# A soft threshold of two VectorE instructions added to the end of the quantiser of the last layer

## The chip, the cores and the metric

One Trainium2 chip, eight cores, one launch. Every core runs the same program on its own batch element; no core waits for another inside the program. The metric is the device time of the slowest core in microseconds.

## The reference

Two layers are applied to x of shape (8, 4096, 1024) in float32, each of them an attention part and a feed-forward part with a layernorm ahead and a residual behind. The change touches the last part alone, the quantised feed-forward of layer 1:

```
def act_quant(x):
    scale = 127.0 / jnp.clip(jnp.max(jnp.abs(x), axis=-1, keepdims=True), 1e-05)
    return jnp.clip(jnp.round(x * scale), -128, 127) / scale
def weight_quant(w):
    scale = 1.0 / jnp.clip(jnp.mean(jnp.abs(w)), 1e-05)
    return jnp.clip(jnp.round(w * scale), -1, 1) / scale
def bit_linear(x, w):
    return jnp.einsum('bsd,hd->bsh', act_quant(x), weight_quant(w))   # forward value

h = bit_linear(x, w1)                       # 1024 -> 4096
h = silu(depthwise_conv1d(h, conv_w, conv_b))   # 3 taps over the sequence
return bit_linear(h, w2)                    # 4096 -> 1024
```

Ahead of it run a gated delta-rule attention, two blocks of local attention with a GELU feed-forward, and an attention over 64 summary tokens. They make up 43.4 ms of the 48.3 and are not touched.

## The kernel before, in words

The activation lies transposed in SBUF, `xf`, 8 chunks of 128 channels by 4096 tokens. The program is a long sequence of blocks; inside a block each engine has its own queue, and the hand-over from one engine to the next goes by counting semaphores: `tick` (a drain and an increment, line 142 stands for the increment of every engine), `wv`, `wt`, `ws` (wait for all that VectorE, TensorE or ScalarE has announced so far) and `wdma` (the same for the DMAs). `b.dma` issues one DMA and then makes the issuing queue wait until it has landed, so there is one DMA in flight on each of the two queues that issue any (SyncE and GpSimd). VectorE runs its own instructions in order, and `v.drain()` between two of them holds the second until the first has left the pipeline.

`_quant7` (lines 2041 to 2055) rounds one 128 by 512 tile. It scales the tile (L2043 by a tile, L2045 by a column), adds and subtracts three large constants (L2047, L2048, L2049), adds and subtracts two of the results (L2051, L2053), and clamps into `out` (L2055). It has three callers in `stage_l1_ffn`, and they run one after the other:

- The weights: for w1T 8 chunks of 8 tiles, for w2T 32 chunks of 2 tiles, 128 calls in all. SyncE loads a chunk into `wch`, for which it waits until VectorE is done with the last one; VectorE quantises all its tiles in place and casts the chunk into the one buffer `wq16s` (L2224); GpSimd stores it to `wr1` or `wr2`. VectorE waits for both the load and the last store before it begins a chunk.
- The activation: 8 windows of 512 tokens, 8 tiles in each, 64 calls, in place in `xf`. Behind them `xf` is cast to bf16 (L2282 to L2287), and the first matrix product with its convolution follows (L2311 to L2360), which writes `ybuf`.
- The hidden layer: 8 windows of 512 tokens, 32 tiles in each, 256 calls. SyncE loads a tile of `ybuf` into one of two buffers, GpSimd loads 128 rows of `wr2` into one of two buffers `w2sl`, VectorE quantises into one of two halves of `yq` in bf16, TensorE does 8 products of 128x128 by 128x512 (L2437) into 8 PSUM banks. VectorE may write a half of `yq` only when the products of two tiles ago are done, and GpSimd has the same rule for `w2sl`. After 32 tiles 8 blocks are scaled, added to the residual and stored (L2461, L2463).

Of the kernel before, what the change touches and what calls it, by code (L numbers as in the profile page):

```python
# [12 lines left out]
ALU = mybir.AluOpType  # L13
# [2024 lines left out]
        b.tick(v, b.sem_v)  # L2038


def _quant7(b, v, w, t1, t2, out, lo, hi, scale_tile=None, scale_col=None):
    if scale_tile is not None:
        v.tensor_mul(w, w, scale_tile)  # L2043
    else:
        v.tensor_scalar(w, w, scale_col, None, ALU.mult)  # L2045
    v.drain()  # L2046
    v.tensor_scalar(t1, w, MAGIC2, MAGIC2, ALU.add, ALU.subtract)  # L2047
    v.tensor_scalar(t2, w, MAGIC3, MAGIC3, ALU.add, ALU.subtract)  # L2048
    v.tensor_scalar(w, w, MAGIC1, MAGIC1, ALU.add, ALU.subtract)  # L2049
    v.drain()  # L2050
    v.tensor_add(w, w, t1)  # L2051
    v.drain()
    v.tensor_sub(w, w, t2)  # L2053
    v.drain()
    v.tensor_scalar(out, w, lo, hi, ALU.max, ALU.min)  # L2055


def stage_l1_ffn(b, xf):
# [143 lines left out]
    for wi, (wname, nch_, cols_, scol, wrh) in enumerate((  # L2202
            ("L1_ffn_w1T", 8, 4096, z.s1col, wr1),
            ("L1_ffn_w2T", 32, 1024, z.s2col, wr2))):
        with nc.Block() as blk:
            for ch in range(nch_):
                @blk.sync
                def _(sy, ch=ch, wname=wname, cols_=cols_):
                    g = b.sg.get("wch", 0)
                    if g:  # L2210
                        sy.wait_ge(b.sem_v, g)
                    b.dma(sy, wch[:, 0:cols_],
                          hb[wname].ap()[ch * 128:(ch + 1) * 128, :])

                @blk.vector
                def _(v, ch=ch, cols_=cols_, scol=scol):
                    b.wdma(v)
                    b.wdma(v, b.sem_g)
                    for sub in range(cols_ // U):
                        _quant7(b, v, wch[:, sub * U:(sub + 1) * U], t1, t2,  # L2220
                                wch[:, sub * U:(sub + 1) * U], -1.0, 1.0,
                                scale_col=scol)
                        v.drain()
                    v.tensor_copy(wq16s[:, 0:cols_], wch[:, 0:cols_])  # L2224
                    b.tick(v, b.sem_v)
                    b.sg["wch"] = b.C.get(b.sem_v)

                @blk.gpsimd
                def _(gp, ch=ch, cols_=cols_, wrh=wrh):
                    b.wv(gp)  # L2230
                    b.dma(gp, wrh.ap()[ch * 128:(ch + 1) * 128, :],
                          wq16s[:, 0:cols_], b.sem_g)
# [6 lines left out]
    for w in range(NCH):  # L2239
        t0 = w * W  # L2240
        with nc.Block() as blk:
# [16 lines left out]
            @blk.vector  # L2258
            def _(v, t0=t0):
                v.tensor_scalar(sct, sct, 1e-5, None, ALU.max)  # L2260
                v.drain()
                v.reciprocal(sct, sct)
                v.drain()
                v.tensor_scalar(sct, sct, 127.0, None, ALU.mult)
                v.drain()
                v.reciprocal(z.mu[:, t0:t0 + W], sct)
                v.drain()
                v.tensor_scalar(z.mu[:, t0:t0 + W], z.mu[:, t0:t0 + W],
                                z.m1col, None, ALU.mult)
                v.drain()  # L2270
                for cc in range(NCH):
                    sl = xf[:, cc * T + t0:cc * T + t0 + W]
                    _quant7(b, v, sl, qt1, qt2, sl, -128.0, 127.0,
                            scale_tile=sct)
                    v.drain()
                b.tick(v, b.sem_v)
# [106 lines left out]
    for w in range(NCH):  # L2383
        t0 = w * W
        with nc.Block() as blk:
# [14 lines left out]
            for hc in range(32):  # L2400
# [18 lines left out]
                @blk.vector  # L2419
                def _(v, hc=hc, bufp=bufp):  # L2420
                    b.wdma(v)
                    g = b.sg.get(("yq", bufp), 0)
                    if g:
                        v.wait_ge(b.sem_t, g)
                    _quant7(b, v, ystg[bufp], qt1b, qt2b,
                            yq16[:, bufp * W:(bufp + 1) * W], -128.0, 127.0,
                            scale_tile=scw)
                    b.tick(v, b.sem_v)
                    b.sg[("ystg", bufp)] = b.C.get(b.sem_v)
# [178 lines left out]
```

How the kernel before makes its waits and increments, by code:

```python
    def dma(self, eng, dst, src, sem=None):  # L131
        sem = self.sem_w if sem is None else sem
        eng.dma_start(dst, src).then_inc(sem, 16)
        self.C.add(sem, 16)
        eng.wait_ge(sem, self.C.get(sem))
# [1 line left out]
    def wdma(self, eng, sem=None):  # L137
        sem = self.sem_w if sem is None else sem
        eng.wait_ge(sem, self.C.get(sem))
# [5 lines left out]
    def wt(self, eng):  # L145
        eng.wait_ge(self.sem_t, self.C.get(self.sem_t))
# [1 line left out]
    def wv(self, eng):  # L148
        eng.wait_ge(self.sem_v, self.C.get(self.sem_v))
# [1 line left out]
    def ws(self, eng):  # L151
        eng.wait_ge(self.sem_s, self.C.get(self.sem_s))
# [257 lines left out]
            @blk.sync  # L410
            def _(sy, wname=wname, j=j, bufp=bufp, sidx=sidx):
                if sidx >= 2:
                    sy.wait_ge(b.sem_t, C.get(b.sem_t) - 1)
                b.dma(sy, slab3(z.wslab, bufp * NCH * 128, NCH, 128),
                      wslab_src(hb[wname], j * 128, 128))
# [342 lines left out]
            @blk.sync  # L758
            def _(sy, j=j, bufp=bufp):
                if j >= 2:
                    sy.wait_ge(b.sem_t, C.get(b.sem_t) - 1)
                b.dma(sy, slab3(z.wslab, bufp * NCH * 128, 4, 128),
                      wslab_src(hb["L0_attn_Wgu"], j * 128, 128))
# [77 lines left out]
            @blk.sync  # L841
            def _(sy, j=j, bufp=bufp):
                if j >= 2:
                    sy.wait_ge(b.sem_t, C.get(b.sem_t) - 1)
                b.dma(sy, slab3(z.wslab, bufp * NCH * 128, NCH, 128),
                      wslab_src(hb["L0_attn_Wo"], j * 128, 128))
```

## Time and profile before

| | us |
|---|---|
| median of the runs of before (two: 48318.64 and 48483.29) | 48400.96 |
| the profiled execution's own time | 48304.51 |
| its span, slowest core (core 2) | 48302.2 |
| spans of all eight cores | 47419.8 to 48302.2 |
| stretch up to the last feed-forward part | 0 to about 43420 |
| quantising the weights | 43614.5 to 44390 |
| quantising the activation | 44390 to 44882 |
| first product and convolution | 44882 to 46782.6 |
| quantising the hidden layer, second product, store | 46782.6 to 48302 |

The profile shows one execution of one core. Busy time is the time in which an engine ran an instruction; the value in square brackets behind a row of the timeline is how long the engine stood idle just before it, with what released it. The time between the starts of two rows that follow each other without such a bracket is the cost of the first one together with its drain.

### The profile page before, as it was taken

The page shows a single profiled execution, that of the slowest core. Times are in us where ns is not written, and L with a number is a line of the kernel's source. Part 1 is how long each engine was busy: PE and PEld are TensorE (multiplying, and loading weights), DVE is VectorE, ACT ScalarE, POOL GpSimd, SP SyncE. Part 2 cuts the span into 40 slices and gives each one's busy share as a digit, 9 for nine tenths or more (in the row PEclk, how much of TensorE's full clock was granted, in tenths as well). Part 3 has the DMA queues.
Part 4 walks back from the last instruction along what each step waited for, and adds up shares of the span by engine and source line. Part 5 has one row for each costly group of instructions (what it writes and reads, how often), then busy time and mean ns, then how long its engine had stood idle before and what let it go on. Part 6 is the DMA issues. An engine that isn't in the chain of part 4 may idle for free. (4 is left out here: it accounts for less than half of the span.)

```text
span 48302.2 us, 310408 instructions; the slowest of 8 cores (47419.8 to 48302.2 us)
## 1 busy us (share of the span) xinstructions
PE 29041.8 (60%) x118094; PEld 17414.8 (36%) x118176; DVE 9809.4 (20%) x17093; ACT 5842.3 (12%) x7328; POOL 230.0 (0%) x420
## 2 busy tenths in 40 slices
PE   5556555655555555577777655557788766640334
PEld 3444444444431111166566211115666642110111
DVE  1222222222122111100000111110000012226556
ACT  0110111111111121211111121111111110000000
POOL 0000000000000000000000000000000000000001
PEclk6666666666666666677877666667777776665666
DMA  1001000000010000033333100002323320011013
GB/s 40 23 20 32 19 25 29 18 28 25 20 35 15 14 10 16 9 84 84 89 84 85 36 11 13 13 11 68 82 79 81 85 82 28 26 54 53 34 59 110
DMA packets 3348641, 2085.22 MB, mean 43 GB/s; under 512 B 169190, under 2 KB 3236075, under 8 KB 3333868
## 3 DMA queue, kind: packets, MB, share of 16 engines
q1 hardware_dynamic: 3309804, 1847.23, 13.8%
q0 software_dynamic: 37376, 218.13, 1.1%
q8 instruction: 963, 15.78, 0.1%
q14 instruction: 498, 4.08, 0.0%
HBM read 1914.11 MB, written 150.99 MB: 43 GB/s over the span
## 5 line engine op out<-in xcount | busy, mean ns | idle before, releaser
L1589 PE MATMUL ps<-pool 128*128 128x256 f32 x11264 | 3962.5, 528 | 2116.5 <-DVEq L142 2116.5
L1589 PEld LDWEIGHTS ps<-pool 128*128 128x128 f32 x11264 | 2966.3, 270 | 3118.8 <-issue 2494.6
L423 PE MATMUL ps<-pool 128*128 128x256 f32 x7168 | 2805.2, 575 | 1458.5 <-DVEq L142 1458.5
L1642 PE MATMUL ps<-pool 128*128 128x256 f32 (+1 forms) x11264 | 3005.8, 433 | 258.7 <-DVEq L142 258.7
L1595 PE MATMUL ps<-pool 128*128 128x256 f32 x11264 | 2927.8, 420 | 0.0
L423 PEld LDWEIGHTS ps<-pool 128*128 128x128 f32 x7168 | 2137.8, 305 | 2127.0 <-issue 1629.7
L1642 PEld LDWEIGHTS ps<-pool 128*128 128x128 f32 (+1 forms) x11264 | 2405.4, 218 | 861.2 <-issue 470.0
L1320 PE MATMUL ps<-pool 128*64 128x256 f32 (+3 forms) x1920 | 1174.8, 712 | 2406.9 <-ACTq L142 2406.9
L1595 PEld LDWEIGHTS ps<-pool 128*128 128x128 f32 x11264 | 2359.5, 209 | 448.1
L1614 DVE SCALAR_TENSOR_TENSOR pool<-ps,pool 128x256 f32<-128x256 f32 x704 | 340.0, 483 | 8326.2 <-ACTq L142 8326.2
L1308 ACT ACT_TABLE_LOAD x960 | 1231.7, 1283 | 5450.4 <-DVEq L142 5450.4
L1607 ACT ACT_TABLE_LOAD x704 | 903.2, 1283 | 7833.6 <-PE ps L1595 7833.6
L1127 PE MATMUL ps<-xf,pool 128*128 128x512 f32 (+1 forms) x2048 | 1322.2, 789 | 618.3 <-DMA pool<-L_ffn_wqkv 376.8
L647 PE MATMUL ps<-pool 64*64 64x64 f32 x10240 | 924.0, 293 | 823.3 <-ACTq L142 673.0
L1320 PEld LDWEIGHTS ps<-pool 128*64 128x64 f32 x1920 | 255.6, 189 | 3144.3 <-issue 3144.3
L2311 PE MATMUL ps<-xq,wsl 128*128 128x512 bf16 x2007 | 623.9, 464 | 1229.8 <-DMA wsl<-wr 1004.7
L197 PE MATMUL ps<-cst_c_id,pool 64*64 64x64 f32 x2560 | 783.1, 306 | 840.3 <-PEq L467 347.9
L1292 PE MATMUL ps<-pool 64*128 64x256 f32 (+3 forms) x1920 | 1205.0, 722 | 129.0 <-DVEq L142 129.0
L198 PE MATMUL ps<-cst_c_id,pool 64*64 64x64 f32 x5120 | 1198.5, 336 | 0.0
L1323 PE MATMUL ps<-pool,cst_c_onescols 128*1 128x256 f32 (+3 forms) x1920 | 1156.8, 704 | 0.0
L647 PEld LDWEIGHTS ps<-pool 64*64 64x64 f32 x10240 | 838.5, 196 | 870.0 <-issue 870.0
L2437 PE MATMUL ps<-yq,w2sl 128*128 128x512 bf16 x2007 | 653.2, 480 | 823.9 <-DVEq L142 728.5
(333 smaller groups left out, 30493.0 us busy)
## 6 DMA issues: line engine op xcount, KB each, us to landing
pool<-L_ffn_w SPq DMA_DIRECT2D x1344, 512.0 KB
pool<-L_ffn_w SPq DMA_DIRECT2D x256, 1344.0 KB
pool<-L_attn_Wq SPq DMA_DIRECT2D x192, 512.0 KB
pool<-L_attn_Wo SPq DMA_DIRECT2D x192, 512.0 KB
pool<-L_attn_Wk SPq DMA_DIRECT2D x136, 512.0 KB
pool<-L_attn_Wv SPq DMA_DIRECT2D x136, 512.0 KB
pool<-L_ffn_wqkv SPq DMA_DIRECT2D x128, 512.0 KB
ybuf<-pool POOLq DMA_DIRECT2D x32, 2048.0 KB, 6.6
```

Of the source, the lines that this page charges most:

```text
L198: return t.matmul(out_ps, src, cid[64:128, 64:128], start=True, stop=True, tile_position=(64, 64))
L423: ins = t.matmul(z.ps_p[:, 0:LT], z.wslab[:, bufp * NCH * 128 + cc * 128:bufp * NCH * 128 + (cc + 1) * 128], z.xn[:, cc * LT:(cc + 1) * LT ...
L647: ins = t.matmul(z.ps_a[PR(h), CB(p)], prevp[PR(h), CB(p)], prevt[PR(h), CB(p)], start=True, stop=True, tile_position=(64 * h, 64 * h))
L1127: ins = t.matmul(out, lh, rh, start=(i == 0), stop=(i == len(mms) - 1))
L1292: ins = t.matmul(pss[:, 0:qn], lhs, rhs, start=True, stop=True)
L1308: s.activation(z.at[:, 0:qn], pss[:, 0:qn], AF.Exp, bias=cst["c_onescols"][:, 4:5])
L1320: t.matmul(z.ps_o[64 * hh:64 * hh + 64, q0:q0 + qn], vsl, z.at[:, 0:qn], start=(kci == 0), stop=last, tile_position=(0, 64 * hh))
L1323: ins = t.matmul(psd[0:1, q0:q0 + qn], cst["c_onescols"][:, 0:1], z.at[:, 0:qn], start=(kci == 0), stop=last)
L1589: t.matmul(z.ps_s0[0:n, 0:ST], wb[:, cc * 128:cc * 128 + n], xn2[:, cc * ST:(cc + 1) * ST], start=(cc == 0), stop=(cc == NCH - 1))
L1595: ins = t.matmul(z.ps_s1[0:n, 0:ST], wb[:, 1024 + cc * 128:1024 + cc * 128 + n], xn2[:, cc * ST:(cc + 1) * ST], start=(cc == 0), stop=(cc ...
L1607: s.activation(z.gsc[0:n, 0:ST], z.ps_s1[0:n, 0:ST], AF.Gelu, bias=z.b1gcol[0:n, lyr * 22 + j:lyr * 22 + j + 1])
L1642: ins = t.matmul(z.ps_o[:, 0:ST], wb[0:n, j * 128:j * 128 + 128], h1sl(j, ST)[0:n, :], start=(j == 0), stop=(j == NJ - 1))
```

## The change

`_quant7` ends in three instructions instead of one. The clamp to lo and hi no longer writes `out` but the work tile `w`. A second clamp of `w`, to plus and minus 2^-14, goes into the scratch tile `t1`, and `out` becomes the difference of the two. Each of the two instructions added has a drain ahead of it. Nothing else is changed: no buffer, no DMA, no wait, no call.

```
+QEPS = 6.103515625e-05
+
+
 def _quant7(b, v, w, t1, t2, out, lo, hi, scale_tile=None, scale_col=None):
@@
     v.tensor_sub(w, w, t2)
     v.drain()
-    v.tensor_scalar(out, w, lo, hi, ALU.max, ALU.min)
+    v.tensor_scalar(w, w, lo, hi, ALU.max, ALU.min)
+    v.drain()
+    v.tensor_scalar(t1, w, -QEPS, QEPS, ALU.max, ALU.min)
+    v.drain()
+    v.tensor_sub(out, w, t1)
```

## Rows read from the trace of the kernel before

**Rows 1.** Page, part 1: busy time (share of the span) xinstructions.

```profile
PE 29041.8 (60%) x118094; PEld 17414.8 (36%) x118176; DVE 9809.4 (20%) x17093; ACT 5842.3 (12%) x7328; POOL 230.0 (0%) x420
```

**Rows 2.** Windows of core 2: stretch, length, busy us (instructions), clock, DMA share, GB/s.

```profile
43614.50:44390.00 775.50, 0.00 (x0) 0.00 (x0) 475.12 (x936) 0.00 (x0) 21.53 (x40) 0.50 0.20 65
44390.00:44882.00 492.00, 39.94 (x112) 16.67 (x112) 399.95 (x658) 0.00 (x0) 0.00 (x0) 0.50 0.00 0
46782.60:48302.00 1519.40, 653.17 (x2007) 213.91 (x2048) 1075.93 (x1960) 0.00 (x0) 178.36 (x320) 0.69 0.37 111
```

**Rows 3.** Timeline of VectorE, weights: start, length, instruction, idle before it.

```profile
43987.99 0.42 DVE L2049 TENSOR_SCALAR pool<-pool 128x512 f32<-128x512 f32 x1
43988.48 0.69 DVE L2051 TENSOR_TENSOR pool<-pool 128x512 f32<-128x512 f32 x1
43989.25 0.69 DVE L2053 TENSOR_TENSOR pool<-pool 128x512 f32<-128x512 f32 x1
43990.01 0.43 DVE L2055 TENSOR_SCALAR pool<-pool 128x512 f32<-128x512 f32 x1
43990.51 0.69 DVE L2224 CAST wq16s<-pool 128x1024 bf16<-128x1024 f32 x1
43996.10 0.48 DVE L2045 TENSOR_SCALAR pool<-pool 128x512 f32<-128x512 f32 x1 [4.89 <-DMA wr<-wq16s]
```

**Rows 4.** Instruction groups of VectorE by form: count, busy us, mean ns, idle before.

```profile
L2053 DVE TENSOR_TENSOR pool<-pool 128x512 f32<-128x512 f32 x384 | 265.9, 692 | 29.6 <-issue 1.3
L2055 DVE TENSOR_SCALAR yq<-pool 128x512 bf16<-128x512 f32 x256 | 109.2, 427 | 20.2 <-issue 0.9
L2055 DVE TENSOR_SCALAR pool<-pool 128x512 f32<-128x512 f32 x128 | 54.6, 427 | 10.5 <-issue 0.9
L2055 DVE TENSOR_SCALAR xf<-xf 128x512 f32<-128x512 f32 x64 | 27.3, 427 | 4.9
L1963 DVE TENSOR_SCALAR xf<-ps,pool 128x512 f32<-128x512 f32 x64 | 48.0, 750 | 543.0 <-PE ps L1953 543.0
```

**Rows 5.** Waits of VectorE in the weights: waited for, us in total, times, longest.

```profile
DVE pool L2045 <- DMA wr<-wq16s: 227.8, 38, 11.2
DVE pool L2055 <- issue: 0.9, 2, 0.4
```

**Rows 6.** Timeline of VectorE, hidden layer, one tile.

```profile
46841.48 0.69 DVE L2043 TENSOR_TENSOR pool<-pool 128x512 f32<-128x512 f32 x1 [0.26 <-issue]
46844.96 0.43 DVE L2055 TENSOR_SCALAR yq<-pool 128x512 bf16<-128x512 f32 x1
46845.64 0.69 DVE L2043 TENSOR_TENSOR pool<-pool 128x512 f32<-128x512 f32 x1 [0.26 <-issue]
```

**Rows 7.** Waits of VectorE in the hidden layer, all eight windows.

```profile
DVE pool L2461 <- DMA outT<-pool: 206.7, 56, 4.8
DVE pool L2043 <- issue: 64.4, 245, 0.6
DVE pool L2461 <- PE ps L2437: 27.4, 8, 4.1
DVE pool L2043 <- PE ps L2437: 2.2, 7, 0.5
```

**Rows 8.** Timeline of GpSimd in the hidden layer: its loads of the weights.

```profile
46883.07 0.55 POOL L133 DMA_DIRECT2D w2sl<-wr  x1 [3.85 <-DMA w2sl<-wr]
46887.21 0.55 POOL L133 DMA_DIRECT2D w2sl<-wr  x1 [3.59 <-DMA w2sl<-wr]
...
46904.31 0.55 POOL L133 DMA_DIRECT2D w2sl<-wr  x1 [3.80 <-DMA w2sl<-wr]
```

**Rows 9.** Timeline of TensorE in the hidden layer: two tiles.

```profile
46908.29 1.89 PE L2437 MATMUL ps<-yq,w2sl 128*128 128x512 bf16 x8 [2.27 <-DVEq L142]
...
46920.77 3.57 PE L2437 MATMUL ps<-yq,w2sl 128*128 128x512 bf16 x8 [1.40 <-DVEq L142]
```

## Prediction

> **What bounds the kernel now.** I read the totals first [rows 1]: TensorE is busy 60% of the span and VectorE 20%. From that alone two more VectorE instructions per tile would look free. The total is a mean over parts with different limits, though, and the change lives in one part only, so the second view is the table of windows, cut where the three callers of `_quant7` begin and end [rows 2]. There the picture is reversed. While the weights are quantised TensorE runs nothing in 775.5 us and VectorE is busy for 475. While the activation is quantised VectorE is busy 400 of 492 us. In the hidden layer VectorE is busy 1076 of 1519 us and TensorE 653. Together the three stretches are 2787 us, 5.8% of the span, and all that the change can do happens in them.
>
> The third view is what VectorE waits for inside each.
>
> Weights: a quantising instruction follows the last one at the drain's distance, then comes the cast, then VectorE stands 4.9 us until the store of that cast has landed [rows 3]. Such waits are 227.8 us over 38 chunks [rows 5]. The store begins when the cast is done, the next quantising begins when the store is done, and the load of the next chunk too is let go only by the cast. So compute, store and compute again stand in a row; nothing runs beside VectorE that would hide a longer chunk.
>
> Activation: no DMA moves at all in that stretch [rows 2], and TensorE only takes part between the windows. It is one chain on VectorE.
>
> Hidden layer: here four queues work side by side, and this is the one place where cover could exist. One tile takes VectorE 4.16 us, from L2043 at 46841.48 to L2043 at 46845.64 [rows 6]. GpSimd's load of `w2sl` comes round in 4.25 us: from 46883.07 to 46904.31 there are 5 steps [rows 8]. TensorE's eight products take 1.89 us at the one clock level and 3.57 at the other, and otherwise it sits waiting for VectorE's tick [rows 9]. VectorE and GpSimd are thus almost even. What decides is which of them waits: VectorE waited for TensorE (through which a late `w2sl` would reach it) for 2.2 us in all [rows 7]. The 0.26 us of idle time ahead of each L2043 has "issue" as its cause, 64.4 us over 245 tiles [rows 7]: the tick and the waits that are already fulfilled. VectorE sets the pace.
>
> **The change, part by part.** It removes nothing: the clamp L2055 stays, with another destination. In the two f32 callers that is the same shape and type as before. In the hidden layer it writes f32 to `pool` in place of bf16 to `yq`; the rows of L2055 show 427 ns for each of the three forms [rows 4], so that edit costs nothing.
>
> It adds a clamp f32 to f32 with constants as limits, the same operation as L2055: 0.427 us. With its drain the distance between two starts is 43990.51 - 43990.01 = 0.50 us [rows 3].
>
> It adds a subtraction of two SBUF tiles. L2053 is just that, 692 ns [rows 4], and with its drain 43990.01 - 43989.25 = 0.76 us [rows 3]. For 192 of the 448 calls it is the same form. For the 256 calls of the hidden layer it writes bf16, a form that has no row. Bounds: at best it runs like the clamp, whose time is the same with bf16 out, 427 ns; at worst like the slowest 128x512 operation that is not a reciprocal, 750 ns with a PSUM source [rows 4]. I take 692, because two f32 sources is what sets L2053 apart from L2055, and a bf16 destination changed nothing for L2055. The ends for the range: 256 x (0.427 - 0.692) = -68 us and 256 x (0.750 - 0.692) = +15 us.
>
> The Trainium skill has a rule for it ("VectorE: DVE Perf Modes", What auto-detection actually checks): the packed two-element mode wants every tensor to be 16-bit, so a subtraction with f32 sources stays at one element a cycle. By that rule the sum is the one that I take; no run here shows it yet.
>
> Per call, from the means: 0.427 + 0.692 busy, and a gap of (29.6 - 1.3)/384 = 0.074 and (20.2 - 0.9)/256 = 0.075 us for the two drains [rows 4], 1.268 us. The starts give 0.50 + 0.76 = 1.26.
>
> - Weights, 128 calls: 162 us. All on the path, for the reason above. Waiting behind VectorE are the store on GpSimd's queue and the load on SyncE's; they are late by the same amount and no longer in themselves.
> - Activation, 64 calls: 81 us, all on the path.
> - Hidden layer, 256 calls: 325 us. A tile goes from 4.16 to 5.43 us. What is late is the tick of `yq`; TensorE, which has 0.6 to 2.3 us to spare per tile, gets more idle time. GpSimd gets 5.43 - 4.25 = 1.18 us of slack per load. SyncE's load of `ybuf` lands while VectorE is at the other buffer. The tail of each window (the last products, eight scaled blocks and stores) is not touched.
>
> Sum: 448 x 1.268 = 568 us.
>
> Small terms: pauses of 0.4 us with "issue" as cause come now and then, ten in the 936 instructions of the weights, of which two stand in [rows 5]. With 256 more instructions there and 512 in the hidden layer this adds some 2 us. At the end of each window VectorE waits for the last products, 27.4 us in eight windows, 4.1 at the longest [rows 7]. The products there run now at the one clock level and now at the other (1.89 us is that of 2.4 GHz, 3.57 that of 1.2) [rows 9], and TensorE will be less busy, 653 us over some 1844 in place of 1519. If the granted clock stays at the lower level throughout, each tail takes the 4.1 us: 8 x 4.1 - 27.4 = 5 us. I take 3.
>
> Sum with them: 573 us. The profiled execution took 48304.5, which gives 48878. The median of the runs is 96 us above that execution and would give 48974. I forecast the middle, 48926 us, a ratio of 1.011 to 1.012 to before.
>
> **Rivals.**
>
> *The subtraction into bf16 runs at the clamp's rate.* For it speaks that nothing in this trace shows the form; against it that L2053's price comes with two sources and not with its destination. 573 - 68 = 505 us: 48858.
>
> *The hidden layer was not bound by VectorE.* For it speaks that GpSimd's 4.25 us is no shorter than VectorE's 4.16; a load at 4.25 would hide 0.09 us a tile at once, 23 us. If each of the 0.26 us ahead of L2043 [rows 6] was in truth a wait for that chain, 64 us of the addition vanish in it: 48862. To hide it all the chain would have to be 5.43 us long, which no row of GpSimd or TensorE is. That would leave 162 + 81 = 243 us: 48597. Against it: 2.2 us of waits for TensorE [rows 7].
>
> *The store and load queue of GpSimd gets slower and becomes the bound (slower by over 2%).* The place is the load of `w2sl` in the hidden layer. Its price is nothing up to a period of 5.43 us, and 256 us for each microsecond beyond that. 2% is 968 us, so 395 us must come on top of 573, and the period would have to reach 6.97 us where it is 4.25. The added clamp is one more instruction of 0.43 us a tile beside it; if it pushed every load back by its whole length, the period would be 4.68 us, and still nothing is late. Time at the deciding point: 49369.
>
> The Trainium skill describes that mechanism ("SBUF — State Buffer", SBUF: two separate sides): while VectorE runs a clamp of this kind GpSimd can't write descriptors, so its DMA starts late. By that rule the loads would be later by up to one clamp, and with the period worked out above the time would stay 48926.
>
> *The subtraction or the clamp is not free of surprises in the drains.* Every drain in the rows costs 0.07 to 0.08 us. At twice that in both, 448 x 0.15 = 67 us more: 48993.
>
> **How the numbers follow.** The forecast has 0.86, the bf16 rate 0.05, a partly or wholly covered hidden layer 0.04, dearer drains 0.03, the GpSimd chain or another doubling of the cost 0.02. The range goes from the cheaper sums on the lower basis to the dearer on the upper one. The low end is 48304.5 + 505 = 48810, less some 20 for the scatter. The high end is 48483.3 (the higher of the two runs) + 573 = 49056, with 15 for a slower subtraction and some 30 for drains: 49100. What is left out is about 1 in 10. 2% is about what a measurement of this kernel can tell from no change, and that is 968 us; the sum is 1.2%, so the case within 2% has 0.96, slower by more 0.03, faster by more 0.01.
>
> **What the profile after would show.** L2055's successor at 427 ns in all three callers; a new TENSOR_SCALAR line x448 at 420 to 427 ns; a new TENSOR_TENSOR line x448 at 692 ns, x256 of them with bf16 out (at 427 the first rival holds). VectorE's total rises by 448 x 1.119 = 501 us to 10311. The three stretches grow by 162, 81 and 325 us, and everything ahead of 43614 keeps its time. The waits for `wr<-wq16s` stay near 228 us and those for `outT` near 207. A tile of the hidden layer takes 5.43 us. I am wrong if VectorE shows new waits for TensorE or DMA there, if the tile stays under 5.2 us, or if the time outside the three stretches moves by more than the runs differ among themselves.

## The result and the profile after

The changed kernel takes 48839 us in the median, the one before 48417; over the runs that can be compared the ratio is 1.0099, with a 95% interval of 1.0061 to 1.0136. So it is slower by about 1%, and less than 2%. The profiled execution of the changed kernel has a span of 48873.3 us, 571 us more than that of before.

First the totals on the page of the changed kernel, the part with the busy times:

```profile
PE 29184.4 (60%) x118176; PEld 17459.6 (36%) x118176; DVE 10314.5 (21%) x17989; ACT 5844.2 (12%) x7328; POOL 232.7 (0%) x420
```

Against [rows 1] VectorE has 896 instructions more, twice 448, and 505 us more of busy time. At 20% and 21% of the span this line alone would never tell that the kernel became slower by it.

The windows of its slowest core (core 1) over the same three stretches; columns as in [rows 2]:

```profile
43637.00:44567.40 930.40, 0.00 (x0) 0.00 (x0) 617.86 (x1193) 0.00 (x0) 20.98 (x39) 0.50 0.16 54
44567.40:45143.00 575.60, 39.95 (x112) 16.73 (x112) 471.56 (x788) 0.00 (x0) 0.54 (x1) 0.50 0.00 1
47027.20:48873.30 1846.10, 790.40 (x2048) 240.43 (x2048) 1363.91 (x2472) 0.00 (x0) 181.05 (x320) 0.62 0.30 91
```

The groups of VectorE for the instructions that are new or have a new destination:

```profile
L2062 DVE TENSOR_TENSOR yq<-pool 128x512 bf16<-128x512 f32 x256 | 177.2, 692 | 19.9 <-issue 0.9
L2060 DVE TENSOR_SCALAR pool<-pool 128x512 f32<-128x512 f32 x384 | 166.0, 432 | 30.6 <-issue 1.3
L2058 DVE TENSOR_SCALAR pool<-pool 128x512 f32<-128x512 f32 x384 | 164.1, 427 | 30.7 <-issue 1.7
```

L2058 is the old clamp, L2060 the clamp to 2^-14, L2062 the subtraction. The subtraction into bf16, the form that had no row before, takes 692 ns like the one into f32.

The end of a call in the weights, VectorE's timeline, to be read against [rows 3]:

```profile
44565.09 0.69 DVE L2056 TENSOR_TENSOR pool<-pool 128x512 f32<-128x512 f32 x1
44565.86 0.43 DVE L2058 TENSOR_SCALAR pool<-pool 128x512 f32<-128x512 f32 x1
44566.36 0.43 DVE L2060 TENSOR_SCALAR pool<-pool 128x512 f32<-128x512 f32 x1
44566.86 0.69 DVE L2062 TENSOR_TENSOR pool<-pool 128x512 f32<-128x512 f32 x1
44567.63 0.69 DVE L2231 CAST wq16s<-pool 128x1024 bf16<-128x1024 f32 x1
```

0.50 us from L2060 to L2062 and 0.77 from there to the cast are what a call got longer by.

A window cut by hand cuts instructions. For the comparisons from here on the stretches are measured on each core from the start of the first VectorE instruction of one part to that of the next: first tile of the weights, first maximum of the activation (L2248), copy ahead of the first product (L2282), first scale of the hidden layer (L2389), end. The means over eight cores, us:

| | until the weights | weights | activation | product, convolution | hidden layer |
|---|---|---|---|---|---|
| before | 43298 | 770.8 | 484.5 | 1850.5 | 1518.5 |
| changed | 43425 | 927.1 | 565.5 | 1856.4 | 1843.5 |
| difference | +127 | +156.3 | +81.0 | +5.9 | +325.0 |

The three stretches grow by 562 us. The other two columns are where the scatter sits. In the profiles below the first one has means from 42708 to 43883 us with the same code in it, its cores from 41723 to 44215, and it goes with TensorE's mean granted clock over the whole span: 0.70 on the cores that are there after 41.7 ms and 0.654 on one that takes 44.2. The 562 us are thus known to some ten microseconds from the stretches, while the ratio of whole runs, 1.0099, has an interval of 295 to 658 us at 48417. The sum of the stretches is inside it. Whole times of single runs below say little for the same reason, and in some of them the cores of one die ran at a lower clock, so the stretches are what is compared.

What VectorE waited for in the hidden layer of the changed kernel, and what GpSimd waited for:

```profile
DVE pool L2468 <- DMA outT<-pool: 207.6, 56, 4.3
DVE pool L2046 <- issue: 65.3, 248, 0.6
DVE pool L2468 <- PE ps L2444: 26.1, 8, 4.0
...
POOL w2sl L133 <- PE ps L2444: 1238.6, 240, 13.5
...
POOL w2sl L133 <- DMA w2sl<-wr: 26.4, 8, 3.6
```

VectorE's waits are those of [rows 7], to a microsecond or two. On GpSimd's queue, in contrast, the picture has turned round. In the kernel before, 228 of the 256 loads of `w2sl` waited for the landing of the last [rows 8]:

```profile
POOL w2sl L133 <- DMA w2sl<-wr: 830.8, 228, 5.2
```

Now GpSimd stands and waits 240 times for TensorE to free a buffer. It has the slack that the prediction gave it.

### The profile page after: what moved, and what is told of

Its sections match the earlier page's. It is cut to its first block and busy times, and to the rows that moved or that the text cites. A ratio compares the mean times of both kernels' runs of the same rounds, so it can differ in the third digit from the quotient of the medians.

```text
span 48873.3 us, 312282 instructions; the slowest of 8 cores (48375.5 to 48873.3 us)
## 1 busy us (share of the span) xinstructions
PE 29184.4 (60%) x118176; PEld 17459.6 (36%) x118176; DVE 10314.5 (21%) x17989; ACT 5844.2 (12%) x7328; POOL 232.7 (0%) x420
## 3 DMA queue, kind: packets, MB, share of 16 engines
q14 instruction: 512, 4.19, 0.0%
## 5 line engine op out<-in xcount | busy, mean ns | idle before, releaser
L2444 PE MATMUL ps<-yq,w2sl 128*128 128x512 bf16 x2048 | 790.4, 555 | 1012.9 <-DVEq L142 991.6
```

## The experiments

**The tail twice.** If the first pass had been partly covered, a second would cost more.

```diff
+    v.tensor_sub(w, w, t1)
+    v.drain()
+    v.tensor_scalar(t1, w, -QEPS, QEPS, ALU.max, ALU.min)
+    v.drain()
     v.tensor_sub(out, w, t1)
```

> The soft threshold (clamp of w to +-2^-14 into t1, subtraction) is done twice in a row in all three callers, so that every quantised value is moved by twice 2^-14 before it is rounded to bf16. Theory (all of the added VectorE time lies on the path that sets the end): each pass costs 1.27 us a call, so against the kernel before the three stretches grow by 2 x 162, 2 x 81 and 2 x 325 us, in sum 1136 us, ratio 1.0235; a tile of the hidden layer takes 6.70 us. Rival (part of the first pass was covered, by GpSimd's load chain or by the waits ahead of a tile): then the second pass costs more than the first, the hidden layer grows by 325 us over the changed kernel but by less than 325 from before to changed. Rival (GpSimd or TensorE becomes the bound): VectorE shows waits for TensorE, tile above 6.8 us.

Stretches 1098.3, 648.5 and 2175.9 us. The second pass adds 171, 83 and 332 us where the first added 156, 81 and 325. From the kernel before the three stretches are 1149 us longer, against the 1136 expected. Per call of the hidden layer that is 1.27 and then 1.30 us.

The second pass thus did cost a little more, as the first rival says, but not because the first was covered. The waits tell where the excess sits, as means over eight cores for before, changed and this run. In the weights VectorE waited 228.3, 220.8 and 227.7 us for the store to `wr`; without that wait the first pass costs 163.8 us and the second 164.3. In the hidden layer it waited 207.3, 204.0 and 206.4 us for the stores to `outT` and 26.8, 28.0 and 30.6 us for the products, which makes the 7 us. Both rivals fall; VectorE still shows no wait for TensorE at a tile's head, only the ticks and the tail of a window (slowest core):

```profile
DVE pool L2046 <- issue: 67.5, 256, 0.6
DVE pool L2472 <- PE ps L2448: 29.0, 8, 4.0
```

The whole times that can be compared, 49565 and 49645 us against 48433, 48460 and 48790 for the kernel before, are too few for an interval; their medians differ by 1145 us.

**The hidden layer alone.** `soft=True` goes only with the third caller; the other two return after the old clamp (that part of the edit is not shown).

```diff
-                            scale_tile=scw)
+                            scale_tile=scw, soft=True)
```

> The soft threshold is added in the hidden layer's caller alone, the weights and the activation end with the clamp as in the kernel before. Theory: hidden layer 1519 + 325 = 1845 us, weights 770 and activation 484.5 us as before; whole time some 325 us above before within the scatter. Rival (the stretches influence each other, for instance by the TensorE clock they leave behind): the product and convolution between them, or the weights, change too by more than the cores differ among themselves.

Weights 781.0 us (cores from 774 to 786, in the kernel before 767 to 776), activation 484.4, product and convolution 1838.2, hidden layer 1843.8. The effect sits where the instructions are; the activation, the product and the hidden layer give no sign of influence. The 10 us of the weights are more than the cores differ, which the rival would ask for, but the weights run ahead of the code that differs from before. They lie in the wait for the store to `wr`, 238.4 us in the mean of the cores where it was 228.3; VectorE's busy time there is the same. Why the stores landed later is open, and the 10 us give the size of what two profiles differ by in that part. The whole time of this single run, 49152 us, is above that of the changed kernel although it does less: its first part took 43883 us in the mean.

**A slower load on GpSimd's queue, before and changed.** This asks directly which queue sets the pace, by making another one slower.

```diff
                     b.dma(gp, w2sl16[bufp][:, :],
                           wr2.ap()[hc * 128:(hc + 1) * 128, :], b.sem_g)
+                    b.dma(gp, w2sl16[bufp][:, :],
+                          wr2.ap()[hc * 128:(hc + 1) * 128, :], b.sem_g)
```

> The kernel before, with GpSimd's load of w2sl in the hidden layer issued twice in a row, each waited for, so that GpSimd's period is about 8.4 us. The result is unchanged. Theory (the pace is set by whichever of the queues is slowest, VectorE at 4.16 us now): VectorE is no longer the bound, it waits for TensorE some 4 us a tile, a tile takes 8.2 to 8.6 us, the hidden layer 2500 to 2650 us, total about 49450. Rival (loads are hidden whatever their length, since there are two buffers): the hidden layer stays at 1519 us.

> The changed kernel with the same doubled load. Theory: in the hidden layer the added 1.27 us a tile now lie inside VectorE's wait of some 4 us, so this stretch takes the same as in the kernel before with doubled load, within 20 us, although VectorE is busy 288 us more; the weights and the activation still grow by 158 and 81 us. Rival (the added work is dear by itself, through its drains or through keeping GpSimd from issuing its loads): the stretch grows by 100 us or more here too.

Windows of the hidden layer, the slower load without and with the soft threshold:

```profile
46695.80:49057.60 2361.80, 886.57 (x2048) 259.11 (x2048) 1078.45 (x1960) 0.00 (x0) 328.51 (x576) 0.59 0.33 100
```

```profile
47173.60:49413.10 2239.50, 883.50 (x2048) 258.88 (x2048) 1365.28 (x2472) 0.00 (x0) 328.19 (x576) 0.59 0.35 105
```

VectorE is busy 287 us more in the second, and the stretch is not longer. Its waits show where that work went, first without and then with the threshold:

```profile
DVE pool L2043 <- PE ps L2439: 662.4, 174, 5.0
DVE pool L2043 <- DMA pool<-ybuf: 159.2, 51, 3.9
...
POOL w2sl L133 <- DMA w2sl<-wr: 1595.4, 496, 4.6
```

```profile
DVE pool L2046 <- PE ps L2446: 336.2, 196, 3.1
DVE pool L2046 <- DMA pool<-ybuf: 42.4, 17, 2.7
...
POOL w2sl L133 <- DMA w2sl<-wr: 1467.3, 496, 4.2
```

So with another queue as the bound the two instructions are free, as the theory has it: 0.43 and 0.69 us are no cost by themselves, only in the place where VectorE is what all wait for. The weights and the activation grew by 157 and 81 us here too.

Two sizes missed. The doubled load gave 2363 us and not 2500 to 2650 (whole time 49125 us, not 49450), since a load then landed in 3.1 us in the median and not in the 3.6 of the kernel before. And the stretch with more work was shorter by 111 us (2251.8 against 2363.2), where 20 at most were expected. That difference is in the landings: GpSimd waited 1595.4 us for them without and 1467.3 with the threshold, 128 us less. Why a load should land sooner when VectorE does more is taken up two experiments below.

**What a drain costs.** Eight more in a row ahead of the last clamp.

```diff
+    for _ in range(8):
+        v.drain()
     v.tensor_scalar(out, w, lo, hi, ALU.max, ALU.min)
```

> The kernel before with eight more drains in a row ahead of the last clamp of each of the 448 calls, and no other instruction. The result is unchanged. Theory A (the 0.075 us between two instructions with a drain is the time in which the first one leaves the pipeline, and a drain on an empty pipeline costs its own 0.01 us or so): 448 x 8 x 0.01 = 36 us more in the three stretches (weights +10, activation +5, hidden +20). Theory B (every drain costs the 0.075 us that the gap shows, so that the two drains make 67 us of the 568 by themselves): +77, +38 and +154 us.

Stretches 816.1, 507.6 and 1610.9: +45.3, +23.1 and +92.4 us. Over 1024, 512 and 2048 drains that is 0.044, 0.045 and 0.045 us each. Neither theory: a drain behind a drain costs 0.045 us, four times what A took and six tenths of B. Part of it are pauses. In most calls the gap ahead of the clamp goes from 0.076 to 0.40 us, which is 0.041 a drain; in 33 of the 448 calls (core 0) it is 0.75 to 0.89. The timeline shows the nine as a gap of 0.40 us:

```profile
47503.27 0.69 DVE L2053 TENSOR_TENSOR pool<-pool 128x512 f32<-128x512 f32 x1
47504.36 0.43 DVE L2057 TENSOR_SCALAR yq<-pool 128x512 bf16<-128x512 f32 x1 [0.40 <-issue]
```

If the one drain behind an instruction costs what a drain behind a drain does, which no run here shows, some 0.09 of the change's 1.27 us a call come from the two drains as instructions, 40 us in all. No run left them out; each instruction reads what the last one wrote.

**Two loads issued together.** The landing times of `w2sl` in the DMA view, kernel before and changed kernel (the last column is the median from issue to landing):

```profile
w2sl<-wr POOLq DMA_DIRECT2D x256, 256.0 KB, 3.6
```

```profile
w2sl<-wr POOLq DMA_DIRECT2D x256, 256.0 KB, 2.9
```

All eight cores have 3.6 in the one and 2.8 or 2.9 in the other. I sorted the 256 loads of `w2sl` by how far SyncE's nearest issue lies from their own. In the kernel before, 139 have one within 0.3 us; in the changed kernel 1 has. To try it, the changed kernel was given back the coincidence:

```diff
+                    g = b.sg.get(("w2s", bufp), 0)
+                    if g:
+                        sy.wait_ge(b.sem_t, g)
                     b.dma(sy, ystg[bufp],
```

> The changed kernel, with SyncE's load of ybuf in the hidden layer made to wait also for the products of two tiles ago, which is what GpSimd's load of w2sl waits for, so that the two loads are issued within 0.3 us of each other. The result is unchanged, VectorE's work is that of the changed kernel. Theory (in the kernel before the load of w2sl lands in 3.6 us because it is issued together with that of ybuf, and in the changed one in 2.9 because the two are released by different engines): the median landing of w2sl goes back to 3.4 to 3.7 us. Rival (it is VectorE's work beside it, of which the changed kernel has more, or the lower load on the memory, since a tile takes 5.4 us and not 4.2): it stays at 2.9 to 3.0. The load of ybuf comes later by up to 3 us here, so VectorE may have to wait for it some 1 us a tile; the time is not what this run is for.

```profile
w2sl<-wr POOLq DMA_DIRECT2D x256, 256.0 KB, 3.3
```

The median goes from 2.9 to 3.3 us (3.2 on the other seven cores) with VectorE's work unchanged. The rival falls. The hidden layer took 1970.9 us, 127 more than in the changed kernel, as VectorE now waits for the later load of `ybuf` (172.3 us on the slowest core). The size is less than the theory's 3.4 to 3.7; the issues here follow each other at 0.46 us (SyncE at 48000.18 and 48005.61, GpSimd at 48000.64 and 48006.07), so they are close but not within the 0.3 us. Sorted by that distance, the mean time from the start of GpSimd's issue to the last packet of its load, us (loads), on the slowest core of each:

| GpSimd's issue against SyncE's nearest | before | changed | this run |
|---|---|---|---|
| within 0.3 | 3.39 (139) | 3.31 (1) | 3.31 (2) |
| 0.3 to 0.5 behind | 3.04 (43) | 2.91 (8) | 2.97 (233) |
| 0.8 to 1.5 behind | 2.91 (35) | 2.61 (13) | 2.79 (7) |
| 0.8 to 1.5 ahead | 2.60 (1) | 2.55 (105) | none |

At the same 0.3 to 0.5 us the kernel before and this run differ by 0.07 us only, although a tile takes 4.19 us in the one and 5.98 in the other; the distance sets most of the landing, and the order counts too. Most of the delay comes ahead of the transfer: the first packet of the 139 comes 1.89 us after the start of the issue, that of the 105 after 1.26. That the coincidence is a cause is shown, that it is the whole of the 0.7 us is not: 0.8 to 1.5 us behind SyncE the kernel before still has 2.91 where the changed one has 2.61, and nothing run here explains that.

The same count answers the question left open above. With the doubled load 109 of 512 loads had SyncE's issue within 0.3 us, and with the threshold added 7.

This also takes some strength from the prediction's near tie. GpSimd's 4.25 us in the kernel before came with two loads in step. In the next run, where VectorE has far less to do and GpSimd's load is what is waited for, its period is 3.97 us in the mean.

**The other direction: fewer instructions.**

```diff
-    v.tensor_scalar(t1, w, MAGIC2, MAGIC2, ALU.add, ALU.subtract)
-    v.tensor_scalar(t2, w, MAGIC3, MAGIC3, ALU.add, ALU.subtract)
     v.tensor_scalar(w, w, MAGIC1, MAGIC1, ALU.add, ALU.subtract)
     v.drain()
-    v.tensor_add(w, w, t1)
-    v.drain()
-    v.tensor_sub(w, w, t2)
-    v.drain()
```

> The kernel before without the two roundings by the larger constants (L2047, L2048) and without adding and subtracting their results (L2051, L2053): for values under 512 both are zero in float32 arithmetic, so what is left out should change nothing. A call gets shorter by 0.34 + 0.34 + 0.76 + 0.77 = 2.21 us, the opposite of the change and larger. Theory (the three stretches are serial on VectorE except that the hidden layer has GpSimd's load right behind it): weights -283 us, activation -141 us, but the hidden layer only down to GpSimd's period of 3.6 to 4.25 us a tile, so -150 to +20 us instead of -566. Total -430 to -580 us, ratio 0.988 to 0.991. Rival (VectorE alone sets the hidden layer): -566 us there, ratio 0.980.

Ratio 0.9921 (0.9885 to 0.9958), just above the 0.988 to 0.991 expected. Weights 500.3 us (-271), activation 343.1 (-141), hidden layer 1441.5 (-77), in sum 489 us less, within the 430 to 580 expected. In the activation the 2.21 us a call come off in full, the mirror image of the change; in the weights 12 us of 283 are missing, and the wait for the store to `wr` is 13.6 us longer (241.9 against 228.3, means). In the hidden layer 2.21 us a call, 566 in sum, were taken out and 77 came back. VectorE now waits there 416.8 us for TensorE, which in turn waits for `w2sl`:

```profile
DVE pool L2043 <- PE ps L2431: 416.8, 195, 4.9
PE ps L2431 <- DMA w2sl<-wr: 337.9, 193, 3.1
```

So the hidden layer's cost is not symmetric. Adding to VectorE costs the whole 1.27 us a tile, taking away gains 0.3, since the next queue stands right behind.

**And that queue relieved.** As the last one, and GpSimd loads the rows for two tiles at once. Of the edit only the load is shown; the two larger buffers, the wait for them and the products' index follow from it.

```diff
+                    if hc % 2:
+                        return
-                    b.dma(gp, w2sl16[bufp][:, :],
-                          wr2.ap()[hc * 128:(hc + 1) * 128, :], b.sem_g)
+                    b.dma(gp, w2d16[wb][:, :].rearrange("p (c n) -> p c n", n=1024),
+                          wr2.ap()[hc * 128:(hc + 2) * 128, :].rearrange(
+                              "(c p) n -> p c n", p=128), b.sem_g)
```

> As e6_short, and in the hidden layer GpSimd loads the weights for two tiles in one DMA of 512 KB into one of two larger buffers, so that there is one wait for a landing in two tiles. Theory: VectorE's bound is gone (about 1.95 us a tile) and GpSimd's too (about 2.5), so SyncE's load of ybuf (2.75 + 0.33 us, one at a time) or TensorE's products (1.9 to 3.6 us) set the pace: 3.1 to 3.7 us a tile, hidden layer 1250 to 1400 us; with -283 and -141 us in the other two, ratio about 0.987. Rival (the load of two tiles lands in twice the time): hidden layer as in e6_short.

Ratio 0.9876 (0.976 to 0.9992), hidden layer 1260.8 us, 258 less than before, the other two as in the last run; in the three stretches 669 us less than before and 1231 less than changed. 512 KB land in 4.4 us where 256 KB landed in 3.3, so one wait for two tiles pays, and the rival falls. The bound has moved once more, to SyncE's load:

```profile
DVE pool L2043 <- DMA pool<-ybuf: 336.3, 214, 3.4
```

This version is faster than the kernel before, by 0.1 to 2.4%; with the changed kernel only its stretches were compared. Its outputs rest on the two roundings that it leaves out being zero, as the expectation says.

## Why the prediction was right, point by point

- *VectorE bounds the three stretches.* Right, and shown from three sides: the stretches grew by 156, 81 and 325 us against 162, 81 and 325; a second pass cost the same again but for 24 us, of which 21 are the waits named above; with a slower queue beside it the work was free. A tile of the hidden layer takes 5.43 us in the median, as forecast. The 6 us too many in the weights are in the wait for `wr<-wq16s`, 227.8 [rows 5] against 221.4, which I had left as it was; a later profile with the weights' clamp unchanged has 10 us more of that wait than the kernel before, so it isn't a finding.
- *The clamp at 427 ns.* 427 for the old one, 432 for the new. The 5 ns come from 30 single instructions of 0.45 to 0.53 us, of which below.
- *The subtraction into bf16 at 692 and not at 427.* Right, 692. The rival of 505 us falls. What the Trainium skill says in "VectorE: DVE Perf Modes", What auto-detection actually checks, is what the row shows.
- *The drains at 0.075 us.* Right as a gap in this place (0.50 and 0.77 us between starts). What it is made of is known in part: a further drain costs 0.041 to 0.045, and whether the first costs as much as an instruction was not measured.
- *Pauses of 0.4 us, some 2 us.* In the weights there are 14 where there were ten. As large as stated.
- *TensorE's clock and the tail of a window, +5 at the most, 3 taken.* The mechanism came, the cost did not. The granted clock in the hidden layer went from 0.69 to 0.62 and the products from 653 to 790 us busy, but VectorE's wait for the last of them is 26.1 us against 27.4 [rows 7]. The term should have been zero.
- *GpSimd's load as the next bound.* Its price of nothing below a period of 5.43 us is right. The rival's cause, a load pushed back by the added clamp, went the other way: it lands 0.7 us sooner.
- *The hidden layer partly covered.* Falls with the waits of VectorE and with the second pass. Its strongest argument, 4.25 against 4.16 us, was a period of two queues in step: over all tiles both have 4.19.
- *The sum.* 573 us predicted; 571 between the two profiled spans, 562 in the three stretches, 423 between the medians, 479 by the ratio. The 571 is partly luck: the part ahead of the change was 23 us longer on the slowest core, and the product with its convolution 17 us shorter. The forecast of 48926 is 87 us above the median measured, inside 48790 to 49100. That the medians differ by 140 us less than the stretches is within the interval of the ratio; the runs show that the first 43 ms scatter by more than that, and no more can be said.

## What to carry to other kernels

An engine that is busy for a fifth of the span can still be where every microsecond counts; cut the trace where the edited code runs and ask what that engine waits for there. If it waits for nothing but its own ticks, the price of an added instruction is its duration with its gap, times the count. The reverse does not hold: what comes back when instructions are removed ends at the next queue, so look at that queue's period first, and at what releases it. Where the rest of the kernel scatters by more than the effect, measure the stretch and not the whole.

## What the runs showed of the hardware that was not expected

Two queues that issue a DMA of 256 KB at the same moment slow down the load of GpSimd, mostly ahead of its first packet, and the step they fall into can hold: 139 of 256 loads within 0.3 us in the kernel before, 1 in the changed one, median landing 3.6 and 2.9 us, and 3.3 when the coincidence was brought back in part.

GpSimd's issue of a DMA and VectorE's clamp can stretch each other where they meet. In the changed kernel, VectorE and GpSimd:

```profile
47099.77 0.51 DVE L2060 TENSOR_SCALAR pool<-pool 128x512 f32<-128x512 f32 x1
```

```profile
47099.50 0.55 POOL L133 DMA_DIRECT2D w2sl<-wr  x1 [5.12 <-PE ps L2444]
47105.01 0.67 POOL L133 DMA_DIRECT2D w2sl<-wr  x1 [4.96 <-PE ps L2444]
```

It takes more than an overlap. In the hidden layer of core 1 a clamp or a rounding (L2050 to L2060) is longer than 0.43 us if it starts 0.24 to 0.32 us after the start of an issue: that holds for 34 of 34, which take 0.45 to 0.53 us and end 0.77 us after the issue's start, and for none of the other 1246, of which many lie beside an issue too. Of the 256 issues 47 take 0.58 to 0.77 us, like the one that the clamps at 47105.13 and 47105.63 overlap, and the others about 0.55. That is the meeting which the Trainium skill describes in "SBUF — State Buffer", SBUF: two separate sides; the longer issues agree with it. By that rule the loads should have come later with one clamp more. Here it is worth 5 ns on the mean clamp, 2 us in all, and the landings became shorter, as the distance to SyncE's issue grew.

The pauses of 0.4 us with "issue" as cause come with the number of instructions, and drains count: the weights have 10 in the kernel before, 14 in the changed one, 19 with the tail twice and 19 with eight more drains a call. What they are no run shows.

A drain right behind another takes 0.041 us of VectorE's time in most calls, and 0.044 to 0.045 with the pauses, the same in all three stretches.
